# Twelve places instead of nine for gathered rows, with a descriptor scratch of 4096 bytes

## What is computed

```python
def _layernorm(x, axis=-1, eps=1e-05): ...

x = x + _L0_gnn_ref(xn, ...) + _L0_mix_ref(xn[None], ...)[0]
x = x + _L0_ffn_ref(_layernorm(x, axis=-1)[None], ...)[0]

def _forward(queries, Wq, bq, keys, w_down, w_up):   # N_HEADS 8, TOP_K 8, N_KEYS 256
    ...
    q = (x @ Wq + bq).reshape(-1, N_HEADS, D_KEYS)
    s1t, i1 = lax.top_k(einsum(q1, keys[:, 0]), TOP_K)
    s2t, i2 = lax.top_k(einsum(q2, keys[:, 1]), TOP_K)
    ...
    scores, best = lax.top_k(all_scores, TOP_K)
    indices = jnp.take_along_axis(all_idx, best, axis=-1)
    w_d = w_down[indices]
    w_u = w_up[indices]
    inner = jnp.einsum('bd,bhkd->bhk', x, w_d)
    vals = jax.nn.relu(inner) * jax.nn.softmax(scores, axis=-1)
    out = jnp.einsum('bhk,bhkd->bd', vals, w_u)
```

## Time and profile before

| | us |
|---|---|
| median of three runs | 2761.16 |
| lowest and highest | 2752.94, 2769.96 |
| span of the profiled execution | 2754.8 |
| first gather of the memory stage in it | 1733.0 |
| TensorE busy | 2409.9 (87%) |
| VectorE busy | 1468.9 (53%) |
| GpSimd busy | 1036.3 (38%) |
| ScalarE busy | 681.1 (25%) |
| software queue (DMAs that GpSimd issues) | 379.99 MB, 42.2% of 16 engines' span |

### The profile page before, as it was taken

The page is one execution under the profiler, slowest core; times in us unless marked ns, Lnnn a source line. Parts: engine busy times, 40 slices in busy tenths (PEclk is TensorE's granted clock), DMA queues, the critical chain, the costliest instruction groups (busy, mean ns, idle before and its releaser), DMA issues.

```text
span 2754.8 us, 27581 instructions
## 1 busy us (share of the span) xinstructions
PE 2409.9 (87%) x9500; PEld 1234.4 (45%) x9500; DVE 1468.9 (53%) x3793; ACT 681.1 (25%) x1687; POOL 1036.3 (38%) x885
## 2 busy tenths in 40 slices
PE   3999989997999999999999987889879879875665
PEld 2656656665444444445656654433333333331210
DVE  3765675455666300002345614477677677677664
ACT  1346231211110011002364211223322332321222
POOL 0066877760111000000000000566666656666665
PEclk9999999998999999999999998999999999987856
DMA  9934145478466601440005000799999989989998
GB/s 304 297 64 127 2 109 117 98 157 223 160 181 196 154 1 52 108 112 19 1 1 172 1 8 8 267 327 342 337 327 342 335 316 348 333 317 340 341 358 313
DMA packets 235969, 524.42 MB, mean 190 GB/s; under 512 B 99362, under 2 KB 99737, under 8 KB 231675
## 3 DMA queue, kind: packets, MB, share of 16 engines
q0 software_dynamic: 170032, 379.99, 42.2%
q1 hardware_dynamic: 57477, 137.07, 16.2%
q10 hardware_dynamic: 8330, 5.71, 0.7%
HBM read 489.51 MB, written 45.34 MB: 194 GB/s over the span
## 4 chain that ended last, share of the span: by engine, by line
PE 67%; DVE 13%; DMA 8%; issue 5%; POOL 3%; another core or an unknown queue 2%; ACT 1%; SPq 0%; DVEq 0%; POOLq 0%; ACTq 0%
PE bank L1070 12%; PE bank L1325 6%; PE bank L1047 5%; PE bank L905 4%; PE bank L916 4%; PE bank L1305 4%; PE bank L1315 3%; PE bank L1259 3%; PE bank L678 3%; PE bank L792 3%; PE bank L570 3%; PE bank L584 2%; PE bank L1057 2%; PE bank L577 2%; DMA qv<-in_L_ffn_rows,qv 2%
## 5 line engine op out<-in xcount | busy, mean ns | idle before, releaser
L1228 POOL DMA_INDIRECT qv<-in_L_ffn_rows,qv x356 | 360.1, 1012 | 1009.4 <-issue 909.0
L1448 ACT ACTIVATE stage<-stage,qv 128x32 f32<-128x32 f32 x640 | 200.3, 321 | 576.8 <-issue 199.0
L1325 PE MATMUL bank<-qv,stage 128*32 128x512 f32 x712 | 257.6, 699 | 91.6 <-ACT stage L1448 48.4
L1612 DVE SCALAR_TENSOR_TENSOR qv<-qv,wreg 128x512 f32<-128x512 f32 x356 | 262.8, 746 | 118.2 <-DMA qv<-in_L_ffn_rows,qv 98.0
L284 POOL DMA_INDIRECT adj<-e_cnt,e_idx x80 | 163.7, 2046 | 193.7 <-issue 176.4
L284 POOL DMA_INDIRECT adj_b<-e_cnt,e_idx x80 | 167.3, 2091 | 62.5 <-issue 35.3
L1305 PE MATMUL bank<-stage,big 128*128 128x250 f32 x640 | 174.2, 399 | 7.5 <-ACT stage L1407 7.5
L1228 POOL DMA_INDIRECT big<-in_L_ffn_rows,qv x142 | 145.8, 1027 | 88.1 <-PE bank L1325 40.5
L1315 PE MATMUL bank<-big 128*125 128x512 f32 x320 | 173.0, 633 | 2.1 <-issue 2.1
L1070 PE MATMUL bank<-big,wreg 125*125 125x512 f32 x400 | 172.0, 592 | 0.0
L1070 PE MATMUL bank<-big,qv 125*125 125x512 f32 x400 | 171.8, 592 | 0.0
(11 more groups left out here) (227 smaller groups left out, 3984.8 us busy)
## 6 DMA issues: line engine op xcount, KB each, us to landing
wreg<-in_L_gnn_basis SPq DMA_DIRECT2D x30, 1024.0 KB
stage<-in_L_gnn_basis POOLq DMA_DIRECT2D x45, 512.0 KB, 4.5
big<-in_L_mix_W SPq DMA_DIRECT2D x4, 4096.0 KB
adj<-adj_b POOLq DMA_DIRECT2D x9, 1328.1 KB, 37.5
adj<-wreg SPq DMA_DIRECT2D x5, 2187.5 KB
adj_b<-wreg SPq DMA_DIRECT2D x5, 2187.5 KB
wreg<-adj SPq DMA_DIRECT2D x10, 1093.8 KB
qv<-adj SPq DMA_DIRECT2D x10, 1093.8 KB
```

The costliest lines, as they stand in the source:

```text
L1228: nc.gpsimd.indirect_dma_start(out=ring[place(t, s)], out_offset=None, in_=a["L0_ffn_rows"], in_offset=bass.IndirectOffsetOnAxis(ap=slots_ ...
L1325: nc.tensor.matmul(psum[7][WIDE * g:WIDE * g + WIDE, :], wsel[:, s % DRING, :], ring[place(t, s)][:, DIM:ROW], start=(s < 4), stop=(s >= S ...
L1448: nc.scalar.activation(wsel[:, s % DRING, :], mask, ACT.Relu, scale=inner[:, s:s + 1]).then_inc(p_diag, 1)
L1612: nc.vector.scalar_tensor_tensor(ring[place(t, s)][:, 0:DIM], ring[place(t, s)][:, 0:DIM], probs_of[t % 2][:, s:s + 1], xrep[:, s % 4, :], ...
```

## The change

`RING` becomes 12, three places of 1024 numbers come from a new tensor `ring_more` of 12288 bytes a partition, and the scratch is set to 4096 bytes, which frees just these 12288 bytes. Everything that is allocated in SBUF moves down in address.

```diff
-RING = 9
+RING = 12
...
         ctx_sb = ctx_flat[:, :].rearrange("p (u d) -> p u d", u=2 * HEADS)
+        ring_more = sb("ring_more", [128, 3 * 1024])
...
-        ring = [region[0:128, at + ROW * n:at + ROW * n + ROW] for region, at, count in ((qv, 5056, 5), (ctx_flat, 0, 1), (stage, 4048, 1), (big, 18384, 2))
+        ring = [region[0:128, at + ROW * n:at + ROW * n + ROW] for region, at, count in ((qv, 5056, 5), (ctx_flat, 0, 1), (stage, 4048, 1), (big, 18384, 2), (ring_more, 0, 3))
                 for n in range(count)]
...
-    nc = bacc.Bacc("TRN2", target_bir_lowering=False, num_devices=1)
+    nc = bacc.Bacc("TRN2", target_bir_lowering=False, num_devices=1, dynamic_dma_scratch_size=4096)
```

## The result

The kernel after takes 2741.5 us (2736.07 to 2747.07) against 2761.16 (2752.94 to 2769.96) for the kernel before: 0.9926 of its time, 95% interval 0.9901 to 0.9952, some 20 us less. Both are medians of five executions (the table of the kernel before says three). The forecast was 2730.0, its range 2703 to 2762. The profiled execution spans 2743.8 us (before: 2754.8).

A forecast was written before the change was run, and what follows sets the result against it. Gathers were taken as mostly limiting the memory stage, with 7 to 9% idle DMA time recoverable. Terms -5 - 10 - 16 = -31 us on 2754.8 gave 2724, plus 6.4 for the median: 2730, range 2703 to 2762.

The forecast's parts named there:

- TensorE and the handshakes are the limit: Rival for the memory stage: only the last tiles' first rows gain, some 8 us, giving 2753 us; chance 0.22.
- Boundaries into tiles 2, 4 and 6, -10 us: At these tile changes VectorE waits 5.5 us for landings; 3.5 us of each should go, bounds 0 and 16.
- tiles 1, 3 and 5, -5 us: At these tiles' starts, rows 8 to 15, TensorE is short of 1.6 us a tile, to be regained; bounds 0 and 13.
- a dot that is late is on the path: Step for boundaries into tiles 2, 4 and 6: TensorE follows the dots through diagonal weights; 3.5 us each claimed.
- Last three tiles, -16 us: In tiles 7 to 9 gathers alone decide; DMA share rising from 0.91 to 0.97 gives 19 us, 16 taken, bounds 0 and 24.
- Stage's DMA share of 0.96: Sign to look for: the DMA engines' share over the memory stage rises from 0.93 to about 0.96.
- GpSimd's waits at tile starts below 1 us: Sign to look for: GpSimd's waits for added rows, 3.83 and 3.44 us at a tile start, shrink below 1 us.
- Indices just in time, 0: At tile changes the next tile's indices come half a microsecond early; nothing charged, 3 us if cover is gone.
- Scratch, 0, with at most 5 us once: Scratch of 4096 bytes costs nothing for gathers; setting back half-base loads behind the ten adding copies could cost some 5 us.
- Everything before 1733 us should stand.: Sign to look for: the program before the memory stage keeps its times; a moved first part would show the prediction wrong.
- 937 us: Time of 640 gathers at the skill page's HBM figure of about 358 GB/s, called some 65 us less than now.
- the boundary term and half of the start terms: Gains at tile changes and starts lost if indices come late: -16 left, giving 2745 us; that rival's chance 0.06.

The follow-up runs named there:

- the first experiment: Nine places as in the kernel before, with the scratch of 4096 bytes and all addresses of the kernel after: 2770.35 against 2767.94 us, ratio 0.9997.
- the light MLP: MLP products on TensorE cut to 32 and 64 columns from 250 and 512, with nine and twelve places: ratios to before 0.9954 and 0.9911.

## Why the prediction was right, and where its steps were not

The time fell inside the range and below no change, some 11 us above the forecast. The same kernel timed again gained 10.8 us instead of 20, which is nearer to the rival "TensorE and the handshakes are the limit" (8 us) than to the forecast (31 us); that the first measurement came so near is in part luck. Against the 31 us of the sum, the stage gained 16.4 us in the profiled execution, and over the traces here 14.6 us: the mean stage is 1026.4 us with nine places (two traces) and 1011.7 with twelve and whole gathers (seven).

- **Boundaries into tiles 2, 4 and 6, -10 us; and tiles 1, 3 and 5, -5 us.** The waits went as said (5.5 to 1.4 us; the text expected some 2). But tiles 0 to 6 together gained 3.7 us in the profiled execution, and 5.7 us in the means (726.2 to 720.5), where nine places alone scatter from 719.8 to 732.5. The step that failed is "a dot that is late is on the path": with 4 us of waits less, the stretch from row 48 of tile 5 to row 7 of tile 6 takes 41.9 us instead of 41.1, and over the stage the waits came back at the search of the next tile. The 1.6 us a tile of rows 8 to 15 came to nothing: these rows take 12.0 us in tiles 1, 3 and 5 of both traces with nine places and all seven with twelve and whole gathers. So the 1.6 us that TensorE lacks there are not made by late rows; I take them for handshakes between its pieces, which no run isolated.
- **Last three tiles, -16 us.** Measured -12.8 in the profiled execution, -9.0 in the means (295.0 to 286.0). Part of it is clear: the last tile, 93.8 to 88.5 us, and no twelve-place trace with whole gathers has more than 89.6. The size was right by the wrong working. The sum kept the busy time of the DMA engines, 302.1 x 0.91 = 275 us, and let the share rise to 0.97; in fact the share stayed at 0.91 and the busy time fell, 289.3 x 0.91 = 263 us, with the same bytes at 341 GB/s instead of 333. The step that was wrong is that idle DMA time is what can be had: the busy time of the engines is no fixed cost of the bytes.
- **Stage's DMA share of 0.96.** Wrong: 0.93 became 0.94. I had read "the pace stays when TensorE's work goes" as a limit in the gathers. In the last tiles the granted clock is 0.71 before and 0.67 after, so TensorE's work per row costs more there; and with half the bytes the stage is no shorter than with twelve places. How much of the stretch is TensorE's own, no run shows. The rival "TensorE and the handshakes are the limit" was the better account of tiles 0 to 6.
- **GpSimd's waits at tile starts below 1 us.** Wrong: they are 3.83 and 3.73 us in tile 5 of after. With three more places GpSimd fills them and stands again. Such a wait says that the ring is full and costs nothing by itself; the landing waits were the ones to read.
- **Indices just in time, 0.** Right: they are never late. The row with 1.39 us names L1563, the copy of the weights, but the gather waits for the index copy alone, which had ended at 2339.45, and GpSimd's gather before ran until 2341.70. Still the first gather of eight of the nine tiles stands 1.36 to 1.39 us here, against 0.31 in all nine of before and also with eleven places; why is open, and it cost nothing that shows.
- **Scratch, 0, with at most 5 us once.** Borne out as far as it can be told: 0.9997 with the scratch alone, but known only to 8 us, so the 5 us are not excluded. The waiting of GpSimd that the text described took place (50.55 us). That the loads behind don't matter was right too: issued ahead of the copies they gained nothing. What was missed is that the copies' crowding is on the path, worth 8 to 9 us in the traces of the copies one by one, and 18.5 us in the medians of the one comparison on a shared chip (by threes).
- **"Everything before 1733 us should stand."** It didn't. The text names a moved first part as a sign of being wrong, and the first gather came 5.4 us later. The adjacency work had begun 8 us later already; whether that is chance isn't shown (see the first experiment).
- **Two loose sums, on which nothing rests.** 937 us are 85 us less than the stage of 1021.8 us (65 is near the difference to the 1005 us of the two windows). And without the boundary term and half of the start terms 18.5 us are left, not 16.

**Open:** why tiles 7 to 9 vary (283.4 to 293.5 us with twelve places), why GpSimd's first gather of a tile stands 1.4 us, and what TensorE alone would allow, since the light MLP changed the clock.

## What to carry to other kernels

A deeper ring takes away waits for landings, but its worth is what the next handshake leaves: sum the waits that vanish (104 us here) and expect a fraction (16 us here) unless every engine behind them is idle for that reason alone. A DMA share of 0.93 beside a busy engine isn't proof that bytes are the limit; halving the bytes can tell. Transfers that nobody waits for soon still set others back when issued in one go, and issuing them by threes gained 18.5 us here, about as much as the three places; one by one and through the smaller scratch gave ratios in the same region (0.9893 and 0.9906).

## What was not expected of the hardware

- Of these adding copies (17 rows of 5000 bytes for each DMA engine), seven are issued into a scratch of 4096 bytes without a stop and three into 2048; the eighth and fourth keep GpSimd standing for 51 and 22 us. The rest of its queue stands with it. Room is not given back copy by copy: in every trace with the copies in one go at 4096 bytes the eighth goes out 0.2 to 0.3 us after the seventh has landed, though the first had landed some 46 us earlier, and at 2048 bytes each group waits for the last of the group before.
- Less work on TensorE made the tiles longer: with narrower MLP products the granted clock fell from 0.94 to 0.74 of the full 2.4 GHz over tiles 0 to 6, a mix of its two levels, and they took 757.5 us instead of 719.8.
- The load of the normalized nodes, 250 KB, took 20.54 us in after and 6.44 us in before, though the graph network's start lay as far behind the copies in both. In after it was issued at 666.97, with the last three copies under way until 678.0; in before at 675.12, when all copies had landed (669.1).
